# A two-layer conditioned attention kernel on one core: a reordered opening, and in the second layer's loop the probability-value groups side by side and both value projections ahead of the first scores

## What is computed

```python
# layer 0: 8 heads of 64, linear attention
q = softmax((xn @ Wq + bq).reshape(b, t, 8, 64), axis=-1)
k = softmax((xn @ Wk + bk + (1 - mask) * -1e6).reshape(b, t, 8, 64), axis=1)
v = ((xn @ Wv + bv) * mask).reshape(b, t, 8, 64)
y = q @ (k^T v)                       # per head
x = x + silu(ln(y) * (1 + scale) + shift) @ W_out + b_out
# layer 1: 16 heads of 32, softmax attention over 128 keys
att = softmax(q k^T + mask term)      # per head, 128 x 128
y = att @ v
out = x + silu(ln(y) * (1 + scale) + shift) @ out_w + out_b
# scale, shift = split(silu(cond_2048) @ W_emb + b_emb)
```

## Time and profile before

| | |
|---|---|
| median of 3 runs | 2180.84 us (2180.38 to 2180.98) |
| the profiled execution's own time | 2180.41 us |
| its span | 2178.6 us |
| PE busy | 2140.4 us (98%) |
| DVE busy | 1400.7 us (64%) |
| ACT busy | 910.7 us (42%) |
| POOL busy | 563.9 us (26%) |

### The profile page before, as it was taken

One profiled execution on the slowest core, in us unless ns is written; L12 is line 12 of the kernel. 1 busy time (PEld: TensorE's weight loads), 2 busy tenths in 40 slices (PEclk: granted clock), 3 DMA queues, 4 the chain that ended last, 5 costly groups with the idle time before them and its releaser, 6 DMA issues.

```text
span 2178.6 us, 53551 instructions
## 1 busy us (share of the span) xinstructions
PE 2140.4 (98%) x20955; PEld 1859.2 (85%) x20955; DVE 1400.7 (64%) x2986; ACT 910.7 (42%) x2088; POOL 563.9 (26%) x890
## 2 busy tenths in 40 slices
PE   6999999999999999999999999999999999999997
PEld 4888888888888888877888888888888888888886
DVE  6777777777777777766564656565555555555554
ACT  3333333333333333442444444444444444445444
POOL 4233333233333233323222212121212121212120
PEclk9999999999999999999999999999999999999999
DMA  6211000111000111103000000000101010101000
GB/s 207 107 39 39 29 34 34 39 39 39 29 34 34 39 39 39 38 21 117 20 29 29 29 29 30 28 36 22 39 19 39 19 39 19 39 19 39 19 31 21
DMA packets 52165, 86.47 MB, mean 40 GB/s; under 512 B 5667, under 2 KB 14565, under 8 KB 52134
## 3 DMA queue, kind: packets, MB, share of 16 engines
q1 hardware_dynamic: 52118, 86.03, 11.2%
q10 hardware_dynamic: 16, 0.00, 0.0%
HBM read 52.32 MB, written 33.69 MB: 39 GB/s over the span
## 4 chain that ended last, share of the span: by engine, by line
PE 94%; DVE 2%; ACT 1%; issue 1%; DMA 1%; SPq 0%; POOL 0%; DVEq 0%; ACTq 0%
PE bank L537 14%; PE bank L538 13%; PE bank L539 13%; PE bank L546 9%; PE bank L547 8%; PE bank L548 8%; PE bank L1650 5%; PE bank L1676 3%; PE bank L1105 3%; PE bank L1682 3%; PE bank L1693 2%; PE bank L1093 2%; PE bank L1006 1%; PE bank L1616 1%; PE bank L1030 1%; PE bank L1034 1%
## 5 line engine op out<-in xcount | busy, mean ns | idle before, releaser
L546 PE MATMUL bank<-xT_hi,w_hi 128*128 128x256 f32 x1536 | 449.1, 292 | 1.1 <-DVE top L1322 1.1
L547 PE MATMUL bank<-xT_lo,w_hi 128*128 128x256 f32 x1536 | 441.1, 287 | 0.0
L548 PE MATMUL bank<-xT_hi,w_lo 128*128 128x256 f32 x1536 | 437.6, 285 | 0.0
L537 PE MATMUL bank<-w_hi,xT_hi 128*128 128x512 f32 x768 | 316.2, 412 | 4.4 <-DVE bias_all L401 4.4
L546 PEld LDWEIGHTS bank<-xT_hi,w_hi 128*128 128x128 f32 x1536 | 291.3, 190 | 19.9 <-issue 8.9
L539 PE MATMUL bank<-w_lo,xT_hi 128*128 128x512 f32 x768 | 307.1, 400 | 0.0
L538 PE MATMUL bank<-w_hi,xT_lo 128*128 128x512 f32 x768 | 304.0, 396 | 0.0
L547 PEld LDWEIGHTS bank<-xT_lo,w_hi 128*128 128x128 f32 x1536 | 291.8, 190 | 1.5 <-issue 0.2
L548 PEld LDWEIGHTS bank<-xT_hi,w_lo 128*128 128x128 f32 x1536 | 292.4, 190 | 0.0
L537 PE MATMUL bank<-w_hi,h_hi 128*128 128x512 f32 x512 | 217.6, 425 | 5.9 <-DVE h_lo L1364 3.7
L926 ACT ACTIVATE heads<-bank,k_neg 128x128 f32<-128x128 f32 x256 | 70.0, 372 | 358.3 <-DVE k_neg L791 358.3
(11 more groups left out here) (210 smaller groups left out, 4053.6 us busy)
## 6 DMA issues: line engine op xcount, KB each, us to landing
xr<-in_x SPq DMA_DIRECT2D x32, 512.0 KB, 3.4
x_between_layers<-ends SPq DMA_DIRECT2D x64, 256.0 KB, 2.0
xr<-x_between_layers SPq DMA_DIRECT2D x32, 512.0 KB, 3.6
out<-ends SPq DMA_DIRECT2D x64, 256.0 KB, 2.0
store<-in_L_cond_W_emb SPq DMA_DIRECT2D x4, 1024.0 KB, 11.4
mask_rows<-mask_parts SPq DMA_DIRECT2D x128, 2.0 KB
heads<-in_L_cond_emb_w SPq DMA_DIRECT2D x2, 1024.0 KB, 7.2
store<-in_L_cond_emb_w SPq DMA_DIRECT2D x2, 1024.0 KB, 11.5
```

Of the source, the lines that this page charges most:

```text
L537: yield nc.tensor.matmul(bank[:, :], a_hi[:, c, b, :], w_hi[:, m, c, :], start=(c == 0), stop=False)
L546: yield nc.tensor.matmul(dst, w_hi[:, m, c, fs], a_hi[:, c], start=(first and c == 0), stop=False)
L547: yield nc.tensor.matmul(dst, w_hi[:, m, c, fs], a_lo[:, c], start=False, stop=False)
L548: yield nc.tensor.matmul(dst, w_lo[:, m, c, fs], a_hi[:, c], start=False, stop=(last and c == C - 1))
```

## The change

In layer 1's body PE does `mixed(i - 1, 0)` and `mixed(i - 1, 1)` one behind the other, weaves the two sets of transposes into query features 2 and 3, and does both value projections before `z_transposed(i - 1, 0)` and `scores(i, 0)`. DVE and ACT follow that order. In the opening the condition is loaded later and turned later, the keys' bias earlier; keys 0 and 2 are projected before the query part; the query bias is waited for one projection later; DVE does the value weight's low part behind the query bias; POOL normalizes pair 1 before its biases, and its three big subtractions are cut in four.

```diff
@@ opening, SP: order of the loads
-    loads = [(cond, T["cond_2048"]),
-             (mask_in[:, 0, :], ...
+    loads = [(mask_in[:, 0, :], ...
+             (m.key_row, T["L0_cond_bk"].rearrange("(o d) -> o d", o=1))]
...
+            if n == K:
+                sp.dma_start(cond, T["cond_2048"]).then_inc(cond_in, 16)
@@ opening, POOL (and the same cut in four in low(n) of layer 1)
-        nc.gpsimd.tensor_tensor(m.w_lo[:, O], raw[O], f32(m.w_hi[:, O]), ALU.subtract).then_inc(s["out_lo"], 1)
+        for c in range(C):
+            nc.gpsimd.tensor_tensor(m.w_lo[:, O, c, :], raw[O][:, c, :], f32(m.w_hi[:, O, c, :]),
+                                    ALU.subtract).then_inc(s["out_lo"], 1)
@@ opening, DVE
         low(Q, range(C))
-        low(V, range(C))
+        dve.wait_ge(tanh_ready, 1)
+        nc.vector.scalar_tensor_tensor(cond_tanh, cond_tanh, 1.0, cond, ALU.add, ALU.mult).then_inc(cond_step, 1)
         yield
         for k, n in ((1, BQ), (2, BV)):
...
+            if n == BQ:
+                low(V, range(C))
@@ opening, PE
-        pe.wait_ge(s["q_bias"], 1)
-        pe.wait_ge(s["split_lo"], 2)
-        yield
+        pe.wait_ge(s["split_lo"], 2)
+        yield
+        pe.wait_ge(s["q_bias"], 1)
         total(2)
@@ layer 1, DVE body
             if not first:
                 end_outputs(i - 1, 0)
+                end_outputs(i - 1, 1)
                 end_norm(i - 1, 0)
-                end_outputs(i - 1, 1)
             values(i, 0, first)
+            if not first:
+                end_norm(i - 1, 1)
+            values(i, 1, first)
             maxima(i, 0, (0,))
             if not first:
                 end_silu(i - 1, 0)
-                end_norm(i - 1, 1)
             maxima(i, 0, (1,))
             if not first:
                 low_part(i - 1, 0)
-            values(i, 1, first)
@@ layer 1, ACT body
             if not first:
                 copy_yT(i - 1, 0)
+                copy_yT(i - 1, 1)
             queries_out(i, (2, 3))
             if not first:
-                copy_yT(i - 1, 1)
@@ layer 1, PE body
                 mixed(i - 1, 0, C + 2)
-            run(projected(i, 0, (2,)))
-            woven(projected(i, 0, (3,)), () if first else turned(i - 1, 0))
-            if not first:
                 mixed(i - 1, 1, C + 4)
-            values0 = value_rows(i, 0, first)
-            run(islice(values0, 4))
-            woven(values0, () if first else turned(i - 1, 1))
+            woven(projected(i, 0, (2,)), () if first else turned(i - 1, 0))
+            woven(projected(i, 0, (3,)), () if first else turned(i - 1, 1))
+            run(value_rows(i, 0, first))
+            run(value_rows(i, 1, first))
             if not first:
                 z_transposed(i - 1, 0)
             scores(i, 0, first)
-            run(value_rows(i, 1, first))
             pe.wait_ge(s["v"], seq(PAIR, i, 1))
             if not first:
                 z_transposed(i - 1, 1)
```

More of the change, by code:

```diff
@@ L288, in high @@
             if n == O:
-                last = nc.scalar.activation(m.w_hi[:, n], raw[n], ACT.Copy)
+                nc.scalar.activation(m.w_hi[:, n], raw[n], ACT.Copy).then_inc(s["split_hi"], C)
             else:
                 for c in range(C):
-                    last = nc.scalar.activation(m.w_hi[:, n, c, :], raw[n][:, c, :], ACT.Copy,
-                                                scale=vcol("L0_cond_ln_w", c))
-            last.then_inc(s["split_hi"], 1)
+                    nc.scalar.activation(m.w_hi[:, n, c, :], raw[n][:, c, :], ACT.Copy,
+                                         scale=vcol("L0_cond_ln_w", c)).then_inc(s["split_hi"], 1)
         def part(k):
@@ L322, in scalar @@
                               f32(rows[pair * PAIR:(pair + 1) * PAIR, 0, :])).then_inc(s["masks_in"], 16)
-        part(0)
+        act.wait_ge(vec_ready, 2)
+        high(K)
         for b in range(PAIR):
@@ L327, in scalar @@
                                  ACT.Copy).then_inc(s["xT_hi"], 1)
+        part(0)
         high(Q)
+        act.wait_ge(cond_in, 16)
+        nc.scalar.activation(cond_tanh, cond, ACT.Tanh, scale=0.5).then_inc(tanh_ready, 1)
         part(1)
@@ L332, in scalar @@
         part(2)
+        act.wait_ge(cond_ps, 1)
+        nc.scalar.activation(m.cond_T[:], ps[6][:, 0:KE * B].rearrange("p (k b) -> p k b", k=KE),
+                             ACT.Copy, scale=0.5).then_inc(cond_ready, 1)
         act.wait_ge(vec_ps, 2)
@@ L376, in vector @@
         dve.wait_ge(vec_ready, 1)
-        low(K, (0,))
         dve.wait_ge(s["rstd"], 1)
@@ L381, in vector @@
                                     ALU.mult).then_inc(s["xn"], 1)
-        low(K, (1, 2, 3))
+        low(K, range(C))
         for b in range(PAIR):
@@ L425, in tensor @@
         last.then_inc(mask_ps, 1)
[L426 to L429, removed]
         pe.wait_ge(mask_step, 4)
@@ L441, in tensor @@
         total(0)
+        pe.wait_ge(s["split_lo"], 1)
+        yield
         pe.wait_ge(mask_off_ready, 1)
         part(1)
-        pe.wait_ge(s["split_lo"], 1)
         yield
-        pe.wait_ge(cond_ready, 1)
         total(1)
         part(2)
+        pe.wait_ge(cond_step, 1)
+        pe.wait_ge(s["xT_lo"], PAIR)
+        for k in range(KE):
+            last = nc.tensor.transpose(ps[6][:, k * B:(k + 1) * B], cond_tanh[:, k * P:(k + 1) * P], m.ident[0:B, 0:B])
+        last.then_inc(cond_ps, 1)
         pe.wait_ge(small_in2, 16 * len(loads2))
@@ L458, in tensor @@
         pe.wait_ge(s["bias_v"], 1)
+        pe.wait_ge(cond_ready, 1)
         pe.wait_ge(s["split_lo"], 3)
@@ L699, in low_parts, with residual @@
                                         ALU.subtract).then_inc(s["h_lo"], 1)
-        def biases(pair, slot, first):
+        def residual(pair, slot):
             pool.wait_ge(s["xn"], seq(PAIR, pair, PAIR))
@@ L706, in biases, with value_bias @@
             last.then_inc(s["x_biased"], 1)
-            if not first:
+        def value_bias(pair, first):
+            if first:
+                pool.wait_ge(s["bias_v"], 1)
+            else:
                 pool.wait_ge(s["v"], seq(PAIR, pair - 1, PAIR))
@@ L725, in body @@
                 next(following)
-            if not first:
+            if first:
+                residual(0, 0)
+                value_bias(0, True)
+            else:
                 low_parts(i - 1)
             if not last:
-                biases(i + 1, (i + 1) % RING, False)
+                residual(i + 1, (i + 1) % RING)
+                value_bias(i + 1, False)
             else:
@@ L1037, in body, with keys, key_biases @@
         def body(i, first, more, last):
-            pe.wait_ge(s["xT_lo"], seq(PAIR, i, PAIR))
-            for f in range(C):
+            def keys(f):
                 dst = ps[f // 2][:, (f % 2) * PAIR * P:(f % 2 + 1) * PAIR * P]
-                if f == 2 and not first:
-                    pe.wait_ge(emb.s["scale"], 1)
                 run(project_features(nc, w_hi, w_lo, K, f, xT_hi, xT_lo, dst, C, True, False))
[L1045 to L1048, removed]
+            def key_biases(f):
+                dst = ps[f // 2][:, (f % 2) * PAIR * P:(f % 2 + 1) * PAIR * P]
                 done = nc.tensor.matmul(dst, key_bias[:, f * P:(f + 1) * P], mask_rows[:, i % RING, :],
@@ L1052, in body @@
                     done.then_inc(s["kT_ps"], 1)
+            pe.wait_ge(s["xT_lo"], seq(PAIR, i, PAIR))
+            if first:
+                keys(0)
+                keys(2)
+                next(start)
+                pe.wait_ge(s["masks_in"], 64)
+                pe.wait_ge(s["key_bias"], 2)
+                key_biases(0)
+                key_biases(2)
+            for f in range(C):
+                if first and f % 2 == 0:
+                    continue
+                if f == 2:
+                    pe.wait_ge(emb.s["scale"], 1)
+                keys(f)
+                if f == 0:
+                    pe.wait_ge(s["masks_in"], seq(32, i, 32))
+                key_biases(f)
             if first:
@@ L1255, in low @@
             pool.wait_ge(s["hi"], (K, Q).index(n) + 1)
-            nc.gpsimd.tensor_tensor(w_lo[:, n], m.raw[n], f32(w_hi[:, n]), ALU.subtract).then_inc(s["lo_qk"], 1)
+            for c in range(C):
+                last = nc.gpsimd.tensor_tensor(w_lo[:, n, c, :], m.raw[n][:, c, :], f32(w_hi[:, n, c, :]), ALU.subtract)
+            last.then_inc(s["lo_qk"], 1)
         norm(0)
```

28 lines of the change are left out of this document (8 added, 20 removed).

## The result

The changed kernel takes 2236.75 us (median of 4 runs, 2230.3 to 2238.4) against 2180.61 for the kernel before; the ratio is 1.0252 with an interval of 1.0231 to 1.0273. It is slower by 56 us.

The account below looks back on a forecast made before the run. PE was taken as the bound, busy 98% of the span and without gaps in layer 1's loop. 2180.4 + 60.5 - 4.5 - 2.5 = 2233.9, stated as 2235; range for 8 in 10: 2222 to 2274 us.

Parts of the forecast that it names:

- The lost cover: Layer 1's loop: z to output projection shrinks to 2.75 us, the chain stays 4.98, so PE waits 2.2 a body.
- The small groups: Layer 1's loop: adjacent probabilities-times-values groups save one entry and one exit, 0.28 us a body, 8.7 in all.
- The net: Layer 1's loop: the new wait less the small groups' saving, 1.95 us a body, 60.5 us slower over 31.
- What is late next: Layer 1's loop: sequence 1's scores and the second output projection wait for nothing; bound 0 to 1 us a body.
- The clock: Rival, chance 0.28: PE's clock also falls in layer 1's loop, 1.7 us each; 2288 if every body, 2261 if half.
- The opening: Before the first query projection: PE's 4.41 us wait goes, 2 to 4 come back; gain 4.5, range 1 to 7.5.
- The end of layer 0: POOL's subtraction cut in four shortens PE's 3.02 us wait; gain 2.5, bounds nothing to nearly 3.0, clock left out.

Follow-up runs that it names:

- value1_back: The changed kernel with the second value projection put back behind the first scores on PE, and its copy put back on DVE; 2159.67 us (0.9902).
- half_between: Like value1_back, but the first six of the second value projection's twelve steps stand ahead of the first scores; 2186.28 us (1.0025).
- z_early: The changed kernel with sequence 0's z transposed between the two value projections, and DVE's SiLU and h_lo moved forward; 2158.34 us (0.9894).
- out_low_late: Like z_early, with POOL's four subtractions for the output weight moved behind the residual and value bias of pair 0; 2151.81 us (0.9871).
- opening_only: The kernel before with all of the change except layer 1's body, which keeps its old order; 2173.57 us (0.9965).
- loop_only: The kernel before with only layer 1's new body; opening as before, POOL's subtractions in one piece; 2242.03 us (1.0281).
- filled_wait: The changed kernel with eight 128x512 matmuls that serve nothing put before PE's wait for h_lo of sequence 0; 2228.68 us (1.0225).

## Why the prediction was right

Forecast 2235, measured 2236.75. The mechanism of the large term is the one that the runs show; that the total came within 2 us is in part luck, as the smaller terms were each off by 2 to 11 us. Step by step:

- *The lost cover.* Forecast: chain 4.98, stretch 2.75, a wait of 2.2 us in 31 bodies. Measured: chain 4.97, stretch 2.70, 2.27 lost. value1_back, half_between and z_early showed that the wait hangs on this alone: by the cover put back, by half a dose and by an earlier start. The bold part of the argument was that no link of the chain gets shorter when PE has less to do; it held.
- *The small groups.* Forecast 0.28 a body, and 0.4 as the bound. Measured against the old loop 0.45 (0.42 by the periods), with z early 0.49. This term was sized too small. I priced one entry and one exit; the halves inside got shorter too (0.87 for 0.90, where I had written 0.90 throughout), and about 0.07 lies in the projections behind them without a name.
- *The net.* Forecast 1.95 a body, measured 1.77: 60.5 against 30 x 1.77 = 53.1 and 2.0 in the last body without its fall of the clock.
- *What is late next.* The scores of sequence 1 and the second output projection waited for nothing in the loop, as forecast; the list of waits has no row for them.
- *The clock.* I gave the falls 0.28 and counted none. There were five in the loop of the profiled run, 7.9 us, and one in its last body, 2.7. So this rival was partly true, at a fifth of the full price of 53, and the clock did not fall anew in each round. It more than made up for the smaller net, which is luck.
- *The opening.* Forecast a gain of 4.5. The first products of the condition start at 48.02, 2.1 us ahead of before; the wait moved to the value projection with its full length, 4.46 for 4.41, and the clock fell behind it as before. This term was too large: I let 2 to 4 us of DVE's delay come back, and all came back. What stayed is the time by which everything ahead of the wait is earlier. The rest was to be had, by moving POOL's work (out_low_late).
- *The end of layer 0.* Forecast 2.5, with the clock left out. The wait of 3.0 is gone whole, and so is the half-rate stretch behind it: by the starts of PE's transposes the changed kernel gains 3.2 us there and 2.4 behind it, 5.6 in all; undoing the cut costs 4.4 us. This term was too small, since the clock was put at nothing although the row of 0.53 was read. The upper bound of the wait was right, and so the sentence on the shared port: DVE loses one piece at most, 1.37 in place of 4.69 for that operation.

So the opening was 2.4 too large and layer 0's end 3.1 too small. In the profiled execution 0.8 came on top within layer 0's ordinary bodies; opening_only's execution does not have it and loop_only's has 0.6, so it is no part of the change. In layer 1, 5.4 too much for the net stands against 10.6 of clock that the sum left out. The large term, the wait, was right by itself.

## What to carry to other kernels

When PE has no gap, the other engines' chains are hidden by exactly what PE does between the matmul that starts a chain and the one that ends it. Before moving work out of such a stretch, add up the chain's links from the trace and compare; the difference is lost once a round, whatever the move was to save. If the order is wanted for another reason, start the chain earlier with it: here the transposes of z moved between the two projections, with DVE's steps moved to fit, turned 56 us lost into 22 gained, 7.5 of which are the opening's and layer 0's.

## What was not expected of the hardware

- Behind a wait of 2.0 us by the list TensorE's clock fell to half, but only in 5 of 30 ordinary rounds of the same loop, and in 3 of 30 in loop_only's profiled execution, where all waits are as long. Each fall made a body 1.57 us longer. Behind waits of 0.6 us a body (half_between) it never fell. The runs of the changed kernel lie between 2230.3, with a mean granted clock of 0.995, and 2238.4, with 0.991; all executions of the kernel before lie between 2179.8 and 2182.2. It does not follow that such waits make a loop less repeatable: loop_only's four lie within 2.1 us, and filled_wait's, with hardly a wait, within 6.1.
- The Trainium skill ("SBUF — State Buffer", section "Who interferes with whom") has the loser of the shared port stand for the winner's whole instruction. The pairs 4.69 beside 4.61 and, with the cut in four, 1.37 in the same place agree with it. But cutting doesn't help a row of DVE operations that all have two inputs in SBUF: four low parts took 6.90 us beside POOL's four pieces, and 7.05 beside the one, against 2.73 alone; POOL's own work took 6.36 us there, where the one instruction took 4.80. A cut shortens the wait of one operation; only a move takes it away.
